# Gated cross-attention and a mixture of experts on one core: running counts in the attention loop, ranks from the matrix product, the output projection ahead of the scores

## The reference

```python
def xattn(Q, K, V):                       # Q = layernorm(x), K = V = context
    q, k, v = Q @ Wq.T + bq, K @ Wk.T + bk, V @ Wv.T + bv     # 16 heads of 16
    attn = softmax(q @ k / 4)
    return (attn @ v) @ Wo.T + bo
x = x + tanh(g_xattn) * xattn(layernorm(x), ctx, ctx)
xf = layernorm(x)
logits = xf @ Wg                          # 16 experts
topi = top_k(logits, 2); gates = softmax over the two
for e in range(16):
    h = silu(xf @ W1[e] + b1[e]) * (xf @ W11[e] + b11[e])
    y = y + (h @ W2[e] + b2[e]) * gates[:, e, None]
z = silu(xf @ Ws1 + bs1) * (xf @ Ws11 + bs11) @ Ws2 + bs2     # shared expert, 1024 wide
x = x + tanh(g_ffn) * (y + z)
```

## Time and profile before

| | |
|---|---|
| three runs | 610.62, 610.73, 611.23 us (median 610.73) |
| the profiled execution's own time | 612.34 us |
| its span from first to last instruction | 610.0 us |
| TensorE busy | 558.2 us, 91% of the span |
| VectorE, GpSimd, ScalarE busy | 57%, 56%, 35% |
| attention, to the last router product | about 208 us |
| shared expert, first half, TensorE busy | to 267 us |
| experts and the shared expert's second half | 276 us to the end |

### The profile page before, as it was taken

One profiled execution on the slowest core, in us unless ns is written; L12 is line 12 of the kernel. 1 busy time (PEld: TensorE's weight loads), 2 busy tenths in 40 slices (PEclk: granted clock), 3 DMA queues, 4 the chain that ended last, 5 costly groups with the idle time before them and its releaser, 6 DMA issues.

```text
span 610.0 us, 11682 instructions
## 1 busy us (share of the span) xinstructions
PE 558.2 (91%) x3146; PEld 443.7 (73%) x3147; DVE 348.0 (57%) x845; ACT 213.5 (35%) x740; POOL 338.8 (56%) x284
## 2 busy tenths in 40 slices
PE   5789889899987999958999999999999999989897
PEld 4356656656655778846888888888888888868786
DVE  5467777777664582213656555655565555322763
ACT  0677776776786111111222222222122222121110
POOL 4477788888879316563444755474444730056620
PEclk9799999999999999988999999999999999989999
DMA  7562000000120602223556787558555210122323
GB/s 250 236 249 85 27 27 18 26 26 17 27 79 18 240 13 93 87 87 124 181 195 201 251 285 254 195 189 296 198 188 209 86 43 27 36 78 77 91 62 115
DMA packets 32319, 76.05 MB, mean 125 GB/s; under 512 B 4896, under 2 KB 21408, under 8 KB 29344
## 3 DMA queue, kind: packets, MB, share of 16 engines
q1 hardware_dynamic: 12944, 51.52, 23.5%
q10 hardware_dynamic: 16272, 15.74, 8.2%
q0 software_dynamic: 3072, 8.39, 4.3%
HBM read 54.93 MB, written 18.61 MB: 121 GB/s over the span
## 4 chain that ended last, share of the span: by engine, by line
PE 70%; DVE 10%; POOL 8%; issue 7%; ACT 2%; DMA 2%; DVEq 0%; ACTq 0%; POOLq 0%
PE mid L646 13%; PE big L627 7%; PE big L629 7%; PE big L628 7%; PE work L402 5%; POOL sorted_x L1332 5%; PE mid L637 3%; PE big L431 3%; PE big L551 3%; PE big L549 3%; PE big L550 3%; PE last L567 3%; PE work L567 2%; PE work L417 2%; PE work L611 2%
## 5 line engine op out<-in xcount | busy, mean ns | idle before, releaser
L774 ACT ACTIVATE last<-arena 128x512 f32<-128x512 f32 x47 | 28.3, 602 | 183.9 <-DVE arena L1142 183.9
L709 ACT ACTIVATE arena<-big,nmax 128x128 f32<-128x128 f32 x256 | 90.3, 398 | 3.7 <-DVE nmax L880 3.7
L646 PE MATMUL mid<-dring,arena 128*128 x376 | 88.9, 379 | 0.0
L627 PE MATMUL big<-u_hi,xsT_hi 128*128 x188 | 82.3, 438 | 0.9 <-issue 0.9
L1142 DVE TENSOR_TENSOR arena<-big,bring 128x512 f32<-128x512 f32 x47 | 32.5, 692 | 87.1 <-PE big L629 87.1
L1251 POOL TENSOR_TENSOR arena<-arena,rinv 128x1024 f32<-128x1024 f32 x32 | 60.7, 1898 | 25.8 <-DVE rinv L888 25.2
L1267 POOL TENSOR_TENSOR u_lo<-arena,u_hi 128x2048 fp32r<-128x2048 f32 x16 | 73.3, 4580 | 1.3
L629 PE MATMUL big<-u_hi,xsT_lo 128*128 x188 | 73.7, 392 | 0.0
L628 PE MATMUL big<-u_lo,xsT_hi 128*128 x188 | 73.3, 390 | 0.0
L646 PEld LDWEIGHTS mid<-dring,arena 128*128 128x128 f32 x376 | 67.8, 190 | 7.4
L709 ACT ACTIVATION_READ_ACCUMULATOR arena<-big,nmax 128x1 f32 x256 | 61.1, 239 | 0.0
(11 more groups left out here) (133 smaller groups left out, 1120.7 us busy)
## 6 DMA issues: line engine op xcount, KB each, us to landing
arena<-up_w_dram SPq DMA_DIRECT2D x16, 1024.0 KB, 7.6
bring<-expert_bias_dram SPq DMA_DIRECT2D x16, 640.0 KB, 5.3
dring<-down_w_dram SPq DMA_DIRECT2D x18, 512.0 KB, 3.4
sorted_y<-arena ACTq DMA_DIRECT2D x47, 128.0 KB, 1.8
arena<-sorted_x ACTq DMA_DIRECT2D x43, 128.0 KB, 2.1
sorted_x<-dring SPq DMA_DIRECT2D x3, 1536.0 KB, 8.4
dring<-up_w_dram SPq DMA_DIRECT2D x2, 1024.0 KB, 4.8
xf_all<-xfs SPq DMA_DIRECT2D x16, 128.0 KB, 2.0
```

Of the source, the lines that this page charges most:

```text
L627: mm(big[:, p, w, :], x_hi, u_hi[:, slot, o:o + HID], start=(k == 0), stop=False)
L646: i = mm(mid[:, 1, 0:D], gT[:, p, c, :], dring[:, slot, c * D:(c + 1) * D], start=(c == 0), stop=(c == HC - 1))
L709: i = nc.scalar.activation(probs[:, u % 2, h, :], big[:, u % 2, h // 4, (h % 4) * CTX:(h % 4 + 1) * CTX], ACT.Exp, bias=nmax[:, u % 2, h:h ...
```

## The change

It moves work within the hand-written orders, computes the positions in another way, and cuts three steps into halves.

- In VectorE's `pair`, `add_attention(j-1, 0)` stands ahead of `row_max` in unit 0, and `ln1_apply(j+2, 0)` moves from unit 2 to the end of unit 1. In TensorE's `pair`, `project_out(j-1, 0)` stands ahead of `scores` in unit 0.
- kT_ready and qT_ready are raised behind each half; the users of the first half wait for that alone.
- A new function `count(j)` adds the two 0/1 rows and keeps a running sum over tiles (three additions). It stands ahead of `choose_copy` in unit 3 of pairs 2 to 7, and at the end for pairs 6 and 7. With it, TensorE makes totals and ranks in three products, and the doubling steps over tiles are gone. The block table is made behind the positions.
- Around this, `shared_up` chunks 2 and 3 of the first group are cut into halves, and the four quarter splits of the shared expert's second half leave POOL's pair 7 and become one split of 2,048 columns ahead of the scatter.

```diff
@@ TensorE, pair
                 for u in range(UNITS):
+                    if behind and u == 0:
+                        pe.wait_ge(lg_taken, j - 1) if not isinstance(j, int) or j > 1 else pe.wait_ge(xnT_ready, j + 2)
+                        project_out(j - 1, 0)
                     if u < 2:
                         scores(j, u + 2)
                     elif ahead:
                         scores(j + 1, u - 2)
-                    if behind and u == 0:
-                        pe.wait_ge(lg_taken, j - 1) if not isinstance(j, int) or j > 1 else pe.wait_ge(xnT_ready, j + 2)
-                        project_out(j - 1, 0)
@@ scores
-                if u == 0:
-                    pe.wait_ge(qT_ready, j + 1)
+                if u < DC:
+                    pe.wait_ge(qT_ready, DC * j + u + 1)
@@ TensorE, behind attention
-            shared_up(0, 2)
+            shared_up(0, 2, [0])
             router(LAST)
-            shared_up(0, 3)
+            shared_up(0, 2, [1])
+            shared_up(0, 3, [0])
             pe.wait_ge(onehots_ready, 1)
-            mm(mid[:, 0, 0:TILES * E], const[:, C_TRI:C_TRI + P], rt[:, 0, :], start=True, stop=True)
-            mm(mid[:, 1, 0:TILES * E], const[:, C_ONE:C_ONE + P], rt[:, 0, :], start=True, stop=True).then_inc(rank_ps, 1)
+            mm(mid[:, 1, 0:E], const[:, C_ONE:C_ONE + P], cum[:, TILES, :], start=True, stop=True).then_inc(totals_ps, 1)
+            mm(mid[:, 0, 0:TILES * E], const[:, C_TRI:C_TRI + P], oh[:, :, :].rearrange("p t e -> p (t e)"), start=True, stop=False)
+            mm(mid[:, 0, 0:TILES * E], const[:, C_ONE:C_ONE + P], cum[:, 0:TILES, :].rearrange("p t e -> p (t e)"),
+               start=False, stop=True).then_inc(rank_ps, 1)
+            shared_up(0, 3, [1])
@@ VectorE, pair (row_max and row_inv stand between the first two pieces)
+                    if behind and u == 0:
+                        add_attention(j - 1, 0)
+                    if behind and u == 1:
+                        add_attention(j - 1, 1)
                     if behind and u < 2:
-                        add_attention(j - 1, u)
+                        ln2_stats(j - 1, u)
+                    if ahead2 and u == 1:
+                        ln1_apply(j + 2, 0)
                     if ahead2 and u == 2:
-                        for b in range(2):
-                            ln1_apply(j + 2, b)
+                        ln1_apply(j + 2, 1)
                     if behind and u == 3:
+                        if not (isinstance(j, int) and j < 2):
+                            count(j - 2)
                         choose_copy(j - 1)
                         choose(j - 1)
@@ new
+            def count(j):
+                link(v.tensor_tensor(oh[:, bass.ds(2 * j, 2), :], chosen[:, 0, bass.ds(2 * j, 2), :],
+                                     chosen[:, 1, bass.ds(2 * j, 2), :], ALU.add))
+                link(v.tensor_tensor(cum[:, bass.ds(2 * j + 1, 1), :], cum[:, bass.ds(2 * j, 1), :], oh[:, bass.ds(2 * j, 1), :], ALU.add))
+                ins = v.tensor_tensor(cum[:, bass.ds(2 * j + 2, 1), :], cum[:, bass.ds(2 * j + 1, 1), :],
+                                      oh[:, bass.ds(2 * j + 1, 1), :], ALU.add)
@@ VectorE, behind attention (ranks; the doubling over tiles and the old positions are removed)
+            dve.wait_ge(totals_ps, 1)
+            link(v.tensor_scalar(cnt[:, 0, :], mid[:, 1, 0:E], P / 2 - 0.5, 1.0 / P, ALU.add, ALU.mult))
+            link(v.tensor_scalar(cnt[:, 1, :], cnt[:, 0, :], ROUND, None, ALU.add))
+            link(v.tensor_scalar(pre[:, 0, PAD:], cnt[:, 1, :], -ROUND, 1.0, ALU.add, ALU.max))
+            while step < E:
+                link(v.tensor_tensor(pre[:, 1 - cur, PAD:], pre[:, cur, PAD:], pre[:, cur, PAD - step:PAD + E - step], ALU.add))
+                cur, step = 1 - cur, 2 * step
+            dve.wait_ge(rank_ps, 1)
+            ins = v.scalar_tensor_tensor(out=r3(0), in0=starts..., scalar=float(P), in1=mid[:, 0, 0:TILES * E]..., ...)
             shared_hidden(0, [3])
+            link(v.tensor_tensor(prod, chosen[:, :, :, :], r3(0).unsqueeze(1).to_broadcast([P, TOPK, TILES, E]), ALU.mult))
+            link(v.tensor_reduce(pos_f..., prod..., AX.X, ALU.add))
+            v.tensor_copy(pos[:, :, :], pos_f[:, :, :]).then_inc(pos_ready, 1)
@@ GpSimd, pair and behind it
-                    if split_first == 1:
-                        pool.wait_ge(raw_odd, 16)
-                        split(PIECES + u, raw_first, 1, u, UNITS)
             keep_xfT(LAST)
+            pool.wait_ge(raw_odd, 16)
+            split(PIECES, raw_first, 1, 0, 1)
             pool.wait_ge(pos_ready, 1)
```

More of the change, by code:

```diff
@@ L535, in _, with shared_up @@
             pair(LAST, 1, False, False, True)
-            def shared_up(s, c):
+            def shared_up(s, c, halves=range(2)):
                 h, g = divmod(s, TILES // GROUP)
                 n = HC * s + c
-                if n >= 2:
+                if n >= 2 and 0 in halves:
                     pe.wait_ge(gsh_ready, n - 1)
@@ L544, in shared_up @@
                 x_lo = [xfT_lo[:, k, GROUP * P * g:GROUP * P * (g + 1)] for k in range(DC)]
-                for w in range(2):
+                for w in halves:
                     for k in range(DC):
@@ L1048, in add_shared @@
                     dve.wait_ge(z_taken, n + 1)
-            for b in range(2):
-                add_attention(LAST, b)
-                ln2_apply(LAST, b)
-                shared_hidden(0, [b])
+            add_attention(LAST, 0)
+            ln2_stats(LAST, 0)
+            count(LAST - 1)
+            ln2_apply(LAST, 0)
+            shared_hidden(0, [0])
+            add_attention(LAST, 1)
+            ln2_stats(LAST, 1)
+            ln2_apply(LAST, 1)
+            shared_hidden(0, [1])
             copy_xfT(LAST)
-            shared_hidden(0, [2])
@@ new lines, in _ @@
+            link(v.tensor_scalar(cnt[:, 1, :], cnt[:, 0, :], ROUND, None, ALU.add))
+            link(v.tensor_scalar(pre[:, 0, PAD:], cnt[:, 1, :], -ROUND, 1.0, ALU.add, ALU.max))
+            cur, step = 0, 1
+            while step < E:
+                link(v.tensor_tensor(pre[:, 1 - cur, PAD:], pre[:, cur, PAD:], pre[:, cur, PAD - step:PAD + E - step], ALU.add))
+                cur, step = 1 - cur, 2 * step
+            ends, starts = pre[:, cur, PAD:], pre[:, cur, PAD - 1:PAD + E - 1]
+            dve.wait_ge(rank_ps, 1)
@@ new lines, in _ @@
+            ins = v.scalar_tensor_tensor(out=r3(0), in0=starts.unsqueeze(1).to_broadcast([P, TILES, E]), scalar=float(P),
+                                         in1=mid[:, 0, 0:TILES * E].rearrange("p (t e) -> p t e", t=TILES), op0=ALU.mult, op1=ALU.add)
+            ins.then_inc(rank_taken, 1)
+            shared_hidden(0, [3])
+            dve.wait_ge(rank_taken, 1)
+            prod = rt[:, 1:1 + TOPK, :].rearrange("p k (t e) -> p k t e", t=TILES)
+            link(v.tensor_tensor(prod, chosen[:, :, :, :], r3(0).unsqueeze(1).to_broadcast([P, TOPK, TILES, E]), ALU.mult))
@@ L1103, in _ @@
             shared_hidden(1, [1])
-            link(v.tensor_tensor(cnt[:, 5, :], ends, cnt[:, 0, :], ALU.subtract))
-            link(v.tensor_tensor(r3(other), r3(cur), r3(1), ALU.subtract))
-            link(v.scalar_tensor_tensor(out=r3(cur), in0=cnt[:, 5, :].unsqueeze(1).to_broadcast([P, TILES, E]), scalar=float(P),
-                                        in1=r3(other), op0=ALU.mult, op1=ALU.add))
-            ins = v.tensor_tensor(r3(other), r3(cur), mid[:, 0, 0:TILES * E].rearrange("p (t e) -> p t e", t=TILES), ALU.add)
-            ins.then_inc(rank_taken, 1)
-            dve.wait_ge(rank_taken, 1)
-            for k in range(TOPK):
-                link(v.tensor_tensor(r3(0), chosen[:, k, :, :], r3(other), ALU.mult))
-                link(v.tensor_reduce(pos_f[:, k, :], r3(0), AX.X, ALU.add))
-            v.tensor_copy(pos[:, :, :], pos_f[:, :, :]).then_inc(pos_ready, 1)
             shared_hidden(1, [2, 3])
@@ L1320, in _ @@
             pair(LAST - 1, True, True, False)
-            pair(LAST, False, True, False, 1)
+            pair(LAST, False, True, False)
             for b in range(2):
@@ L1338, in _ @@
             pool.wait_ge(sh_ps, HC * TILES // GROUP)
[L1339 removed]
+            split(PIECES + 1, raw[:, 0, :], 0, 0, 1)
             pool.wait_ge(table_ready, 1)
```

74 lines of the change are left out of this document (33 added, 41 removed).

## The result

| | before | after |
|---|---|---|
| median of five runs | 610.73 us | 613.41 us |
| lowest and highest | 607.94, 611.23 | 612.83, 614.40 |
| the profiled execution's own time, its span | 612.34, 610.0 us | 612.83, 611.0 us |

The medians differ by 2.7 us, a ratio of 1.0044; the estimate from the runs is 1.0058 (3.5 us), with a 95% interval of 1.0037 to 1.0080. So the changed kernel is slower, by some 3 us, where 4.7 less were forecast. The time is in the range (598 to 614) and in the rival "case B in every pair" (611.7 to 615).

A forecast was written before the change was run, and what follows sets the result against it. TensorE is 91% busy; VectorE sets the loop, GpSimd pair 7, late pos the wait for sorted rows. -6.0 + 6.8 - 2.5 - 3.0 = -4.7 us gives 607.6 profiled, 606.0 for the median; range 598 to 614, forecast's own 602 to 609.

The forecast's parts named there:

- case B in every pair: Rival: loop additions lose each race with xfT_lo; 611.7 to 615 us; chance 0.28 for slower by over 0.2%.
- the toss-up in the counts: Unit 3 of the loop: whether the third count addition gets in ahead of GpSimd's xfT_lo; +6.8 us taken.
- case A: Third count addition gets in ahead of xfT_lo; `chosen` ends 0.6 us later than before; taken for three pairs.
- case B: xfT_lo starts first, third count addition waits for it; `chosen` ends 2.5 us later; taken for two pairs.
- B throughout: Upper bound of the loop's counts: xfT_lo first in all five pairs, 5 x 2.5 = 12.5 us; whole kernel 614.
- order and halves, six pairs: Attention loop, pairs 1 to 6: earlier addition to x_all and half-wise queries save about 1.0 us a pair, -6.0 us.
- counts in the loop: Additions held by GpSimd delay logits and `chosen`, five times ahead of pair 7; +6.8 us, bounds 0 to 12.5.
- pair 7: End of attention: quarter splits leave the way between GpSimd's normalisations; -2.5 us, bounds 0 and 5.7.
- last router product to the first rows and behind: Attention to first expert block: earlier pos removes TensorE's wait for sorted rows and its slow stretch; -3.0 us.

The follow-up runs named there:

- e13: Kernel before with only the loop's moves and halves: no counts, no new ranks, splits still in pair 7; 604.27 us.
- e6: Changed kernel with the four quarter splits back in GpSimd's pair 7, counts still with two inputs; 606.69 us.
- e3: Changed kernel with the count additions, in the same place, written as reductions with one SBUF input; 596.12 us.
- e11: Changed kernel with one-input reductions for the counts and the four quarter splits back in GpSimd's pair 7; 595.36 us.
- e1: Changed kernel with all 24 count additions behind the last choice and none in the loop; 607.05 us.
- e2: Changed kernel with the output projection of unit 0 behind the scores again in TensorE's order; 612.76 us.
- e5: Changed kernel with the split of 2,048 columns cut into quarters, one behind each of the four groups of scatter transfers; 612.95 us.
- e9: Changed kernel with the three additions written as scalar_tensor_tensor, still two SBUF inputs; 616.03 us in one run.
- e12: Changed kernel, two-input counts, with two, one and one quarters of the split behind the first three groups of scatter transfers; 607.41 us.

## Why the prediction was wrong

**The step that failed is the toss-up in the counts**, "I take A for three pairs and B for two: 1.8 + 5.0 = +6.8 us"; measured were +11.4 us. That held additions delay the logits was right, and so was the order named for the first two: the first waited to the end of the normalisation, the second to that of xfT_hi. But in pairs 1 to 4 the third was issued behind the start of xfT_lo, by 0.03, 0.02, 0.03 and 0.10 us, and waited for it each time: case B four times, case A never. I had both delays, 0.18 and 0.17 us, from the earlier trace rows, and they said that it loses; nothing in the rows spoke for a pair in which it wins. From e13 to after the periods of pairs 2 to 5 grow by 2.28, 2.26, 2.26 and 2.16 us, 9.0 in the sum (2.5 each were worked out for case B).

The fifth set of additions, at the end of pair 5, was a second error. I had argued that GpSimd's queue, written out from there, favours B. In fact the copy that I had put ahead of the additions is missing in that pair, the first addition came before the normalisation and none met xfT_lo: neither A nor B. The period of pair 6 grew by 2.43 us all the same. Three things add up in it. The hold costs 2.0 us (e6 against e13, 19.33 and 17.37 us, both with the splits in pair 7 and with the clock at its upper level in this pair); the missing splits give back about 0.9 (e3 against e11); what is left, about 1.3 us, I put down to the clock, which fell behind the wait of 1.69 us at the projection. So the total of 11.4 is near the 12.5 of "B throughout" in part by luck. The prediction named the rule of the Trainium skill, page SBUF — State Buffer, section SBUF: two separate sides, beside the toss-up, and by it every pair was B; it says that whoever starts first holds the port for the whole instruction. Pairs 1 to 4 agree (third addition at 87.18, xfT_lo at 87.15), and so does pair 5, where the order was another.

The bookkeeping, term by term, from the starts of the profiled executions:

| term | predicted | measured | from |
|---|---|---|---|
| order and halves, six pairs | -6.0 | -5.0 | e13 against before, router 0 to router 6 |
| counts in the loop | +6.8 | +11.4 | after against e13, the same stretch |
| pair 7 | -2.5 | -2.4 | 11.38 against 13.80 us |
| last router product to the first rows and behind | -3.0 | -2.6 | -0.2 to the rows, -2.4 from there to VectorE's last operation |
| sum | -4.7 | +1.4 | |

The start of the loop came 0.6 us sooner (first router product at 62.91 instead of 63.46), which with 0.1 us behind VectorE's last operation leaves 1.0 us between the profiled spans; the own times differ by 0.5 us. The medians differ by 2.7, since the profiled execution of before lay 1.6 us above the median of its runs and that of after 0.6 below: a reason to compare medians, and to read single terms under 2 us from starts within one trace.

**Order and halves.** 1.0 us a pair was right for the first four; it overstated pairs 5 and 6, where the loop's chain is another.

**Pair 7.** The size was right partly by luck. Only 1.1 to 1.2 of the 2.4 us come from the splits (e11 against e3, e6 against after). The rest is the router, which now stands ahead of a half chunk of `shared_up`: with the splits still in pair 7 it takes 12.43 us in e11 and 13.78 in e13. The splits' other 0.9 us lie in pair 6, in the row of the counts. The counts in pair 7 itself cost nothing, though held (11.38 us, and 11.36 in e1 without them).

**The end.** Here the mechanism was as predicted. `chosen` and the first count ended with operations of the split; the wait at the totals was 5.47 us (5.6 predicted), the clock was low behind it, and the wait for the sorted rows was gone. But pos came 7.8 us behind the counts (5.9 predicted), because the silu of chunk 3 was done 5.5 us behind them instead of 3.3, and so pos was only 0.7 us nearer to the last router product than before. The rows came 3.2 us later than before, not sooner, because the loop's delay came on top. What the prediction did not work out is that these terms hide a bad trade: with sums that nothing holds, ranks by TensorE and what goes with them are worth 8.9 us (e11 against e13), and with the two-input sums the split's new place alone costs 6.7.

**The wait at the projection** was not foreseen. In pairs 1 to 4 it cost nothing of its own (e2); behind that of pair 5 the clock fell, as said above.

## What to carry to other kernels

Where a VectorE operation with two SBUF inputs can meet a GpSimd operation that reads SBUF, take its cost as the rest of that operation, once for every link of a dependent chain, and don't bet on a gap of 0.17 us between two of them. Then look for a form that isn't held (here a reduction over two values side by side) or for a place ahead of the operation that releases GpSimd; either was worth 9 to 17 us here. And when a wait moves, read what stands behind it in each queue: the split's place decided when four weight loads went out in front of the loads that TensorE was waiting for.

## What the runs showed that I had not expected

- A copy of 4 columns, `top` (one SBUF input), took 0.81 us at 89.52 in the changed kernel and 0.52 in the median, against 0.17 in the median before. It ends with the GpSimd operation beside it (89.26 to 90.30); so one input is no safeguard for every operation, while the reductions of e3 were never held. The same section of the Trainium skill's page SBUF — State Buffer says that a copy can enter a mode that takes the shared port pair and a reduction can't. No run here varied the copy.
- Four waits of 2.19 to 2.35 us ahead of `project_out` left TensorE's clock at its upper level (1.13 us for the four products at 88.72), and a shorter one of 1.69 us was followed by the lower one (2.07 us for the same products at 183.72, granted clock 0.56 from 183.7 to 187.4). In e6 it was the other way round: the clock fell behind the first wait of 2.28 us (1.88 us for the products at 88.27, granted clock 0.54 to 92.0), and behind a wait of 1.71 us the products took 1.13 us at 184.50. In e5, e9 and e12 it fell behind the first wait, at about 90, and again behind the one of 1.69 us. A fall behind the first wait made the second period 25.1 us instead of 23.9. The length of one wait did not tell which. It also means that differences of about 1 us between these kernels can be the clock.
